# Second feed-forward with tokens sorted by expert through DRAM, and seven query-key products moved from GpSimd to VectorE

## Chip, cores and metric

The kernel runs on one core of a Trainium2 chip. The metric is the device time of one launch in microseconds, the median of three runs. TensorE (PE in the profile) multiplies matrices into PSUM banks, VectorE (DVE), ScalarE (ACT) and GpSimd (POOL) work elementwise, and SyncE (SP) issues the transfers. Each engine runs its own instruction list in order and meets the others at semaphores.

## The reference, cut to what matters

`x` holds 32 tiles of 128 tokens with 128 features, 4096 tokens in all. Eight residual steps follow each other: attention 0, feed-forward 0, attention 1, feed-forward 1, token attention, feed-forward 2, attention 3, feed-forward 3. The change concerns feed-forward 1 (eight experts of width 352, of which each token uses its best two) and, since they now stand beside it differently, token attention (16 heads of one token attend to each other) and feed-forward 2.

```python
# feed-forward 1, on layernorm(x): E = 8, I = 352, TOP_K = 2
logits = jnp.einsum('th,eh->te', xf, w_router)
probs = jax.nn.softmax(logits, axis=-1)
topw, topi = jax.lax.top_k(probs, TOP_K)
topw = topw / jnp.sum(topw, axis=-1, keepdims=True)
combine = jnp.einsum('tk,tke->te', topw, onehot)
gate = jax.nn.silu(jnp.einsum('th,eih->eti', xf, w_gate))
up = jnp.einsum('th,eih->eti', xf, w_up)
down = jnp.einsum('eti,ehi->eth', gate * up, w_down)
out = jnp.einsum('eth,te->th', down, combine)
# token attention, on layernorm(x): 16 heads of width 8, causal over the heads
scores = jnp.einsum('bsqd,bskd->bsqk', qh, kh) / math.sqrt(hd)
attn = jax.nn.softmax(jnp.where(mask, scores, -1e18), axis=-1)
out = jnp.einsum('bsqk,bskd->bsqd', attn, vh)
# feed-forward 2, on layernorm(x): 128 -> 512 -> 128, hidden layer and w2 rounded to fp8
```

## The kernel before

All of x stays in SBUF. Work goes in 32 tiles of 128 tokens, taken in 8 groups of 4 tiles (512 tokens). The order is written out by hand: each engine's block in `program` is one list, with a loop over pairs of groups for the middle of each stage (`walk`), and every hand-over is a wait on a counted semaphore.

Feed-forward 1 is dense. Its 8 x 352 = 2816 hidden units are cut into 22 chunks of 128 (`NC1`), and every group of 512 tokens goes through all 22 chunks, 176 chunks in all. For a chunk TensorE forms the gate (line 1199) and the up product (1205), each 512 columns in fp32, and adds the four 128x128 down products of the chunk two before (`finish`, 1181) into a bank that holds the group's sum. ScalarE applies silu (845), VectorE multiplies the two (`hide`, 1664). The router's weights come in by scaling the input of the up product (`shared`, 1654), or the hidden units where a chunk spans two experts (1672); their rows go through the DRAM tensor `share_rows` and come back broadcast over the partitions.

Token attention for the tiles of the group before runs between the chunks, at fixed slots of the 22 (`SCORE_SLOTS` and the like). For one tile GpSimd forms the query-key products (`products`, 647, four instructions), VectorE adds them up and prepares the softmax (`score`, 1727 to 1737), ScalarE takes the exponential (829), VectorE divides (`probabilities`, 1741 to 1747), GpSimd forms the products with the values (`weighted`, 660), and VectorE adds them into x (`combine`, 1753 and 1758). There is one buffer for each kind of products, so GpSimd may form the next tile's only once the last ones are read. GpSimd also does the two small operations of every inverse deviation (506, 508).

The last four tiles of token attention run in `feed_forward2`, one beside each of its groups 0 to 3. One group there is: `norm_stats` (1351, 1356) and `norm` (1374) on VectorE, four transposes (1122), four 512-column products (1225), `rectify` on ScalarE (867), sixteen fp8 products (1233), and two VectorE operations that add the result (1779, 1784). Groups 4 to 7 follow, with the start of attention 3 between them: its projections, the split of queries and keys into bf16 parts on GpSimd (515 to 529), and 18 transfers of those parts from SyncE's queue (377, 381), on which its first scores (964) wait.

Of the kernel before, what the change touches and what calls it, by code (L numbers as in the profile page):

```python
# [50 lines left out]
NC1 = E * I1 // P  # L51
EXPERTS1 = [((P * c) // I1, (P * c + P - 1) // I1) for c in range(NC1)]
MIXED = [c for c in range(NC1) if EXPERTS1[c][0] != EXPERTS1[c][1]]
FIRST1 = [min(c for c in range(NC1) if EXPERTS1[c] == (e, e)) for e in range(E)]
# [15 lines left out]
for _name, _len in (("bv0", 128), ("bv1", 128), ("bv3", 128), ("bo1", 128), ("bo3", 128), ("b_ffn0", 128),  # L70
                    ("b2_ffn2", 128), ("gate_b", E), ("first_wins", E), ("heads_causal", H * H)):
    ROWS[_name] = (_at, _at + _len)
    _at += _len
# [8 lines left out]
def waits_apart(eng):  # L82

    eng.nop(nofuse=True)
# [23 lines left out]
def program(nc, x_in, ctx_in, ctx_t, mask0, mask3, w_attn, w_ffn0, w_router, w_gate, w_up, w_down, w1, w2, gate3,  # L108
            mlp1, mlp2, mlp2_b, cols_in, rows_in, consts_in, pick_in, out):
    with ExitStack() as ctx:  # L110
# [3 lines left out]
        def sem(name):  # L114
# [57 lines left out]
        room = sb("room", [P, 2 * E * I1 + E * 3 * P])  # L172
        xn_all = room[:, 0:NT * P]
        wg = room[:, 0:E * I1]
        wu = room[:, E * I1:2 * E * I1]
        wd = room[:, 2 * E * I1:3 * E * I1].rearrange("p (c d) -> p c d", c=NC1)
# [20 lines left out]
        ctx_tok = [work[2 + b][:].rearrange("p (t d) -> p t d", t=TG) for b in range(2)]  # L197
        xq = h3
# [9 lines left out]
        hidden1 = [area[:, GT * i:GT * (i + 1)] for i in range(4)]  # L208
        xw = [area[:, GT * (4 + i):GT * (5 + i)] for i in range(2)]
        share = [q_rows[h][:].rearrange("p s n -> p (s n)").bitcast(F32).rearrange("p (e n) -> p e n", e=E // 2)  # L210
                 for h in range(2)]
        share_mixed = [ctxT[:, 0, :], ctxT[:, 1, :], xnT[:]]
        share_rows = nc.dram_tensor("share_rows", (2, E, GT), F32, kind="Internal").ap()
        zeros_b = sb("zeros_b", [P, P], BF16)
        comb1 = [sb(f"comb1{b}", [P, E, TG]) for b in range(2)]
# [21 lines left out]
            chunk_down xw_ready share_stored""".split()  # L237
# [9 lines left out]
         product_ready, lin_taken, x_first, x_second, rows_loaded, lin_ready, pick_loaded, chunk_down,  # L247
         xw_ready, share_stored) = (sem(n) for n in names)
        share_loaded = [sem(f"share_loaded{h}") for h in range(2)]
# [1707 lines left out]
```

## Time and profile before

| | us |
|---|---|
| median of three runs (1754.88 to 1757.84) | 1756.35 |
| the profiled execution: its own time | 1759.78 |
| the profiled execution: span, first to last instruction | 1757.7 |
| busy of the span: PE, DVE, ACT, POOL | 80%, 75%, 41%, 39% |

A profile describes one execution. "Busy" leaves out waiting and the issue of transfers. A view of windows gives each engine's busy time in a stretch; a timeline row gives start, duration, engine, line, operation and, in brackets, how long the engine had been idle and what released it; a view by line groups all instructions of a source line. The fp32 matmuls count as two instructions each ("x8" is four products of 128 columns).

### The profile page before, as it was taken

The numbers are of one execution on the slowest core, as the hardware profiler recorded it, in microseconds if no ns is written. First come the engines' busy times: TensorE is split into PE (matmuls) and PEld (weight loads), VectorE is DVE, ScalarE is ACT, GpSimd is POOL, SyncE is SP. The second block draws the span as 40 slices with busy tenths as digits, with TensorE's granted clock in tenths as the row PEclk, the third lists the DMA queues.
The fourth block names the chain that finished last, engine by engine and source line by source line (L and its number), as shares of the span: only waits on it lengthen the run. The fifth ranks groups of instructions, "written<-read, shape, count | busy, mean of one in ns | idle before, by whom it ended". The sixth has DMA issues, their size and how long they took to land. (4 is left out here: it accounts for less than half of the span.)

```text
span 1757.7 us, 32824 instructions
## 1 busy us (share of the span) xinstructions
PE 1407.4 (80%) x10456; PEld 897.4 (51%) x10456; DVE 1318.4 (75%) x3282; ACT 727.7 (41%) x1306; POOL 690.7 (39%) x718
## 2 busy tenths in 40 slices
PE   3888883489989998988988989565589897878787
PEld 1555552256666565554545545333266664455454
DVE  5768776676767569889788897877467564899898
ACT  1455552156656324334333343232166564333333
POOL 0223211023341024445354454454024431687786
PEclk9999996599999999999999999877699998899899
DMA  8455530364532221020220211000554450000000
GB/s 187 66 81 69 70 49 1 44 159 66 73 49 37 91 84 68 29 79 22 80 68 24 84 35 64 12 1 1 101 69 68 60 69 5 1 13 1 13 12 12
DMA packets 73205, 92.98 MB, mean 53 GB/s; under 512 B 7984, under 2 KB 59952, under 8 KB 70448
## 3 DMA queue, kind: packets, MB, share of 16 engines
q1 hardware_dynamic: 73072, 91.36, 26.6%
q8 instruction: 65, 1.06, 0.3%
q14 instruction: 68, 0.56, 0.1%
HBM read 51.35 MB, written 2.23 MB: 30 GB/s over the span
## 5 line engine op out<-in xcount | busy, mean ns | idle before, releaser
L1400 DVE TENSOR_REDUCE neg_max<-bank 128x4 f32<-128x512 f32 x384 | 252.7, 686 | 149.5 <-PE bank L966 147.7
L764 ACT ACTIVATE probs<-bank 128x512 f32<-128x512 f32 x384 | 212.3, 596 | 169.8 <-PE bank L993 169.0
L1181 PEld LDWEIGHTS bank<-room,area 128*128 128x128 f32 x1408 | 188.6, 195 | 83.9 <-issue 80.2
L845 ACT ACTIVATE work<-bank 128x512 f32<-128x512 f32 x176 | 105.1, 597 | 292.1 <-PE bank L1199 246.7
L964 PE MATMUL bank<-mask_b,ident_b 128*128 128x512 bf16 x384 | 155.9, 406 | 76.0 <-DMA k_rows<-area 50.5
L506 POOL TENSOR_SCALAR rstd_a<-meanvar 128x4 f32<-128x4 f32 x64 | 15.9, 249 | 457.9 <-DVE meanvar L1356 371.4
L660 POOL TENSOR_TENSOR prod<-mask_i,work 128x128 f32<-128x128 f32 (+3 forms) x128 | 133.7, 1075 | 157.9 <-DVE mask_i L1747 157.9
L1181 PE MATMUL bank<-room,area 128*128 128x128 f32 x1408 | 189.5, 279 | 0.0
L1199 PE MATMUL bank<-xT,room 128*128 128x512 f32 x352 | 183.0, 602 | 0.0
L1664 DVE TENSOR_TENSOR area<-work,bank 128x512 f32<-128x512 f32 x176 | 119.2, 682 | 56.7 <-PE bank L1205 50.5
L1205 PE MATMUL bank<-area,room 128*128 128x512 f32 x256 | 134.7, 608 | 28.4 <-DVE area L1664 16.8
L966 PE MATMUL bank<-k_rows,q_rows 96*128 96x256 bf16 x768 | 156.6, 287 | 0.0
L757 ACT ACTIVATE q_rows<-bank 32x512 bf16<-32x512 bf16 x192 | 103.0, 582 | 120.6 <-PE bank L976 116.9
L983 PE MATMUL bank<-ident_b,mask_b 128*128 128x512 bf16 x384 | 134.9, 393 | 3.0 <-ACT probs L764 1.8
L993 PE MATMUL bank<-q_rows,k_rows 128*128 128x128 bf16 x1536 | 135.9, 222 | 0.0
L647 POOL TENSOR_TENSOR probs<-h,work 128x128 f32<-128x128 f32 (+3 forms) x128 | 120.0, 967 | 23.4 <-DVE probs L1727 13.0
L993 PEld LDWEIGHTS bank<-q_rows,k_rows 128*128 128x128 bf16 x1536 | 112.5, 100 | 27.8 <-issue 2.2
L1007 PE MATMUL bank<-probs,v_aug 128*32 128x128 f32 x3072 | 112.9, 288 | 0.8
L515 POOL CAST area<-area 128x1024 bf16<-128x1024 f32 x19 | 19.7, 1036 | 227.6 <-DMA k_rows<-area 170.2
L966 PEld LDWEIGHTS bank<-k_rows,q_rows 96*128 96x128 bf16 x768 | 78.6, 102 | 54.0 <-issue 11.2
L585 POOL TENSOR_TENSOR probs<-probs,work 128x512 f32<-128x512 f32 x64 | 82.5, 1289 | 50.1 <-DVE probs L1854 50.1
L1205 PEld LDWEIGHTS bank<-area,room 128*128 128x128 f32 x256 | 46.7, 191 | 99.8 <-issue 42.4
(182 smaller groups left out, 2789.2 us busy)
## 6 DMA issues: line engine op xcount, KB each, us to landing
q_rows<-area SPq DMA_DIRECT2D x144, 128.0 KB
k_rows<-area SPq DMA_DIRECT2D x288, 64.0 KB
q_rows<-share_rows SPq DMA_DIRECT2D x16, 1024.0 KB, 4.6
ctxT<-ctx_t SPq DMA_DIRECT2D x24, 256.0 KB, 7.7
ctxT<-share_rows SPq DMA_DIRECT2D x32, 128.0 KB, 3.7
ctxT<-share_rows SPq DMA_DIRECT2D x16, 192.0 KB, 3.6
xnT<-share_rows SPq DMA_DIRECT2D x16, 192.0 KB, 3.5
mask_i<-mask SPq DMA_DIRECT2D x8, 256.0 KB, 8.5
```

Of the source, the lines that this page charges most:

```text
L647: ins = pool.tensor_tensor(prod[:, at:at + 4 * nj * DH].rearrange("p (i j d) -> p i j d", i=4, j=nj), q[:, 4 * i:4 * i + 4, :].unsqueeze(2 ...
L660: ins = pool.tensor_tensor(prod2[:, at:at + 4 * nj * DH].rearrange("p (i d j) -> p i d j", i=4, d=DH), tok_p[:, 4 * i:4 * i + 4, 0:nj].uns ...
L764: act.activation(probs[j].rearrange("p a b -> p (a b)"), T_BANK[j % 2][:], ACT.Exp).then_inc(exp_done, 1)
L964: pe.matmul(dst[:], ident_b[:], bcast(mask(b, t), 4), start=True, stop=False)
L966: mm = pe.matmul(dst[:, 256 * i:256 * i + 256], q_rows[b][SCORE_ROWS, 2 * j + i, tok], k_rows[b][SCORE_ROWS, :, 2 * j + i, tok], start=Fal ...
L983: pe.matmul(T_BANK[j % 2][:], mask(b, t), bcast(ident_b[:], 4), start=True, stop=False)
L993: mm = pe.matmul(dst[:, i * P:(i + 1) * P], k_rows[b][:, j % 2, hp, tok], q_rows[b][:, hp, tok], start=False, stop=i == 3)
L1181: mm = pe.matmul(dst[:, t * P:(t + 1) * P], hidden1[(c + 2 * b) % 4][:, t * P:(t + 1) * P], wd[:, c, :], start=False, stop=c == NC1 - 1 an ...
L1199: pe.matmul(S_BANK[c % 2][:], wg[:, P * c:P * (c + 1)], xT[b][:], start=True, stop=True).then_inc(gate_filled, 1)
L1205: pe.matmul(T_BANK[c % 2][:], wu[:, P * c:P * (c + 1)], xT[b][:] if mixed else xw[e % 2], start=True, stop=True).then_inc(up_filled, 1)
L1400: dve.tensor_reduce(neg_max[:, 4 * j:4 * j + 4], S_BANK[j % 2][:].rearrange("p (h k) -> p h k", h=4), AX.X, ALU.max, negate=True).then_inc ...
L1664: ins = dve.tensor_tensor(h, work[c % 2][:], T_BANK[c % 2][:], ALU.mult)
```

## The change

Feed-forward 1 computes only the two chosen experts of each token. The tokens are taken in 4 chunks (`NCH`) of 8 tiles (1024 tokens, 2048 token-expert pairs). For a chunk:

- `route_stats`, `route_norm`, `logits` and `choose` (VectorE, TensorE) find the two experts and, after a tanh on ScalarE, the weights; `ranks` counts with 17 bf16 products, for each pair, how many earlier pairs have the same expert; `put` turns that into the row of each pair and into the expert of each block, in some twenty small VectorE steps.
- `scatter` (GpSimd) writes the normalised rows into the DRAM tensor `moe_rows` with 16 indirect transfers of 128 rows of 512 bytes. Each expert's rows begin at a multiple of 128, so 24 blocks of 128 rows (`NBLK`) always suffice, 96 for all chunks (`NB`). `clear_rows` zeroes the tensor beforehand, 6.3 MB, in four transfers issued at the start of feed-forward 0.
- `sorted_rows` (SyncE) loads four blocks at a time (a quad, 24 steps in all) and stores the results over them. Per block TensorE transposes the rows (one of the quad's four), forms gate and up with the tokens as weights and the expert's 352 columns as the moving side, transposes the hidden units in three pieces and forms three down products. The expert is read into a register once a quad and sets the address of the weights.
- `gather` (GpSimd) fetches for each group two rows per token with 8 indirect transfers, and `add_taken` (VectorE) adds them to x with the weights, 8 instructions.

Token attention starts at step 9 of the 24 (`FIRST_STEP`), one tile a step: tiles 0 to 14 beside the blocks, tiles 15 to 31 behind them. For tiles 1, 3, 5, 7, 9, 11 and 13 (`ON_DVE`) VectorE forms the query-key products itself. Feed-forward 2's groups 0 to 6 stand beside the tiles 15 to 30, group 7 behind the last tile. The start of attention 3 now stands beside tiles 21 to 23; its split is made by VectorE, and its 18 transfers are issued then. This part is written out without loops.

```diff
+UNITS = [(0, P), (P, P), (2 * P, I1 - 2 * P)]
+TC = 2 * TG
+NCH = NT // TC
+QUAD = 4
+NQ = 6
...
+FIRST_STEP = 9
+ON_DVE = [n for n in range(NK - FIRST_STEP) if n % 2]
...
+        FFN2_STATS = {15: 0, 16: 1, 17: 2, 18: 3, 20: 4, 24: 5, 28: 6}
+        FFN2_NORM = {16: 0, 17: 1, 18: 2, 19: 3, 21: 4, 25: 5, 29: 6}
+        FFN2_ADD = {17: 0, 18: 1, 19: 2, 20: 3, 22: 4, 26: 5, 30: 6}
+        NEXT_STATS = {21: 0, 22: 1}
+        NEXT_NORM = {22: 0, 23: 1}
...
+            def sorted_rows():
+                sp.wait_ge(t_filled, 8 * NT)
...
+                def load(k):
+                    if k % NQ == 0:
+                        sp.wait_ge(scattered[k // NQ], 16 * 2 * TC)
+                    if k >= 4:
+                        sp.wait_ge(blk_turned, k - 3)
...
+            def scatter(c):
+                pool.wait_ge(placed, c + 1)
...
+                for o in range(2 * TC):
+                    t = o // 2
+                    pool.indirect_dma_start(
+                        moe_rows, bass.IndirectOffsetOnAxis(place_i[:, c, o:o + 1].bitcast(mybir.dt.uint32), 0),
+                        rows_of(c, t // TG)[:, t % TG, :], None).then_inc(scattered[c], 16)
...
+                at = 3 * NG
+                for n in range(NT):
+                    g, t = divmod(n, TG)
+                    if n + 1 < NT:
+                        products(n + 1)
+                    for events in (FFN2_STATS, NEXT_STATS):
+                        if n in events:
+                            at += 1
+                            inv_std(at)
+                    weighted(n)
+                    if g + 1 < NG:
+                        if t < 2:
+                            gather(g + 1, range(2 * t, 2 * t + 2))
+                        if t == 2:
+                            token_std(g + 1)
...
+                def experts(k):
...
+                    four = pe.value_load(expert_i[0:1, c, q:q + 1], min_val=0, max_val=E ** QUAD - 1)
...
+                    pe.matmul(S_BANK[i % 2][:, 0:I1], tokens, room[:, bass.ds(weights_at[k, m], I1)], start=True, stop=True
+                              ).then_inc(gate_filled, 1)
...
+                for n in range(NK - FIRST_STEP, NT):
+                    score(n)
+                    combine_last(n)
+                    between(n)
+                    if n in FFN2_ADD:
+                        ffn2_add(FFN2_ADD[n])
+                    if n in FFN2_NORM:
+                        ffn2_norm(FFN2_NORM[n])
...
+                    probabilities(n)
+                    if n == 23:
+                        for part in range(4):
+                            attention(2, True, part)
+                combine(NT - 1)
+                norm_stats(NG - 1, NT, tok_written)
+                ffn2_norm(NG - 1)
+                ffn2_add(NG - 1)
...
             def score(n):
 
-                dve.wait_ge(tok_products, n + 1)
+                if n in ON_DVE:
...
+                        ins = dve.tensor_tensor(
+                            prod[:, at:at + 4 * nj * DH].rearrange("p (i j d) -> p i j d", i=4, j=nj),
+                            q[:, 4 * i:4 * i + 4, :].unsqueeze(2).to_broadcast([P, 4, nj, DH]),
+                            k[:, 0:nj, :].unsqueeze(1).to_broadcast([P, 4, nj, DH]), ALU.mult)
```

In the order of the instructions, three places. First TensorE, one chunk of the dense stage before (`bank` is PSUM, `room` the experts' weights, `area` hidden units or scaled tokens):

```order
L1199 MATMUL bank<-xT,room 128x512 [waits gate_act]
L1205 MATMUL bank<-area,room 128x512 [waits hidden_ready]
L1181 MATMUL bank<-room,area 128x128 [waits hidden_ready]
L1181 MATMUL bank<-room,area 128x128 x3
```

and the start of a quad with one block now:

```order
L1302 TENSOR_LOAD m2b
L1302 ISA x2
L1313 REGISTER_ALU [waits gate_act,blk_taken]
L1313 ISA
L1313 MATMUL bank<-room,area 128x352
L1317 ISA [waits hidden_ready]
L1317 MATMUL bank<-room,area 128x352
...
L1325 MATMUL bank<-ident,area 128x128 [waits hidT_taken,hidden_ready]
L1325 MATMUL bank<-ident,area 128x128
L1325 MATMUL bank<-ident,area 96x128
L1334 ISA [waits hidT_taken]
L1334 MATMUL bank<-room,area 128x128
```

Two long products and four short ones of a chunk became two shorter long ones, three transposes and three short ones of a block, with an address instruction (ISA) ahead of each product and a load of the quad's experts ahead of its first.

Second GpSimd, between two tiles of token attention, before:

```order
L647 TENSOR_TENSOR probs<-h,work 128x512
L506 TENSOR_SCALAR rstd_a<-meanvar 128x4 [waits stats_ready]
L508 TENSOR_TENSOR rstd<-rstd_a,minus_half 128x4 [waits pool_steps]
L660 TENSOR_TENSOR prod<-mask_i,work 128x128 [waits tok_summed,tok_probs]
```

and now, at tile 16:

```order
L556 TENSOR_SCALAR rstd_a<-meanvar 128x4 [waits stats_ready]
L558 TENSOR_TENSOR rstd<-rstd_a,minus_half 128x4 [waits pool_steps]
L748 TENSOR_TENSOR prod<-mask_i,q_rows 128x128 [waits tok_summed,tok_probs]
...
L748 TENSOR_TENSOR prod<-mask_i,q_rows 128x512
L595 DMA mask_b<-moe_rows,m2b 128x128 [waits x_mixed,blk_stored0,blk_stored1]
L595 DMA mask_b<-moe_rows,m2b 128x128 x3
L734 TENSOR_TENSOR probs<-h,q_rows 128x128 [waits tok_scored,xq_ready]
```

Four indirect transfers stand between the products of one tile and the next, at two of every four tiles.

Third VectorE, at tile 18, where one tile, the gathered rows of group 5 and a group of feed-forward 2 meet:

```order
L2058 TENSOR_REDUCE mask_i<-prod 128x32 x3
L2063 SCALAR_TENSOR_TENSOR x<-mask_i,gates,x 128x128 [waits tok_summed]
L1885 SCALAR_TENSOR_TENSOR x<-mask_b,m2b,x 128x128 [waits gathered5]
...
L1894 BN_STATS m2b<-x 128x6 [waits x_mixed]
...
L2010 TENSOR_TENSOR o<-bank,b_q 128x512 [waits x_written,down_filled]
L2014 SCALAR_TENSOR_TENSOR x<-o,gates,x 128x512 [waits down_read]
L1510 TENSOR_SCALAR xn<-x,meanvar,rstd 128x128 [waits rstd_ready,f_filled]
...
L2046 TENSOR_REDUCE mask_i<-probs 128x16 [waits tok_exp]
```

Before, x got the dense stage's sum in one instruction a group (line 1678); the eight of line 1885 take its place.

## Rows read from the trace of the kernel before

**Rows 1.** Windows by stage: start:end, length, busy (instructions) per engine, PEclk, DMA.

```profile
333.50:576.60 243.10, 209.24 (x2381) 144.30 (x2382) 166.16 (x425) 137.87 (x281) 66.23 (x75) 0.92 0.43 76
...
576.60:1127.30 550.70, 492.72 (x2213) 303.26 (x2211) 453.77 (x1006) 195.02 (x282) 242.70 (x253) 0.98 0.17 56
...
1127.30:1242.00 114.70, 61.30 (x246) 34.49 (x246) 82.79 (x217) 32.55 (x50) 52.13 (x60) 0.73 0.03 8
```

**Rows 2.** Timeline of TensorE in the dense stage: start, us, engine, line, count.

```profile
704.71 1.05 PE L1181 MATMUL bank<-room,area 128*128 128x128 f32 x8
705.60 1.02 PE L1199 MATMUL bank<-xT,room 128*128 128x512 f32 x2
```

**Rows 3.** VectorE by line, 576 to 1127 us: count, busy us, mean ns, idle before.

```profile
L1664 DVE TENSOR_TENSOR area<-work,bank 128x512 f32<-128x512 f32 x176 | 119.2, 682 | 56.7 <-PE bank L1205 50.5 <-issue 2.9 <-PE bank L1181 1.2
...
L1727 DVE TENSOR_REDUCE probs<-probs 128x16 f32<-128x128 f32 (+1 forms) x112 | 46.4, 475 | 4.2 <-POOL probs L647 4.2
...
L1753 DVE TENSOR_REDUCE mask_i<-prod 128x32 f32<-128x128 f32 (+1 forms) x108 | 44.8, 476 | 15.0 <-POOL prod L660 15.0
...
L1732 DVE TENSOR_TENSOR probs<-probs,rows 128x256 f32<-128x256 f32 x28 | 27.6, 986 | 1.0
...
L1737 DVE TENSOR_TENSOR probs<-probs,mask_i 128x256 f32<-128x256 f32 x28 | 27.1, 966 | 1.0
...
L1747 DVE TENSOR_TENSOR mask_i<-probs,mask_i 128x256 f32<-128x256 f32 x28 | 11.9, 425 | 1.4 <-DVE mask_i L1743 0.5
...
L1735 DVE TENSOR_REDUCE mask_i<-probs 128x16 f32<-128x256 f32 x28 | 11.8, 420 | 1.0
...
L1741 DVE TENSOR_REDUCE mask_i<-probs 128x16 f32<-128x256 f32 x28 | 11.6, 413 | 0.0
...
L1758 DVE SCALAR_TENSOR_TENSOR x<-mask_i,gates,x 128x128 f32 (+1 forms) x27 | 9.5, 352 | 1.0
...
L1743 DVE RECIPROCAL mask_i<-mask_i 128x16 f32<-128x16 f32 x28 | 7.1, 253 | 1.0
```

**Rows 4.** Timeline around the last group of feed-forward 2.

```profile
1218.38 0.60 PE L1122 MATMUL bank<-ident,xn 128*128 128x128 f32 x4
...
1229.82 1.11 PE L1122 MATMUL bank<-ident,xn 128*128 128x128 f32 x4 [5.43 <-DVE xn L1374]
...
1241.28 0.75 DVE L1784 SCALAR_TENSOR_TENSOR x<-o,gates,x 128x512 f32<-128x512 f16 x1
...
1258.36 0.58 PE L964 MATMUL bank<-mask_b,ident_b 128*128 128x512 bf16 x1 [13.10 <-DMA k_rows<-area]
```

**Rows 5.** The page: busy tenths of the 16 DMA engines in 40 slices.

```profile
DMA  8455530364532221020220211000554450000000
```

**Rows 6.** Timeline of SyncE's queue: a DMA issue.

```profile
350.04 0.44 SPq L413 DMA_DIRECT2D room<-w_down  x1
```

**Rows 7.** DMA issues: count, KB each, us to landing.

```profile
work<-ctx_in SPq DMA_DIRECT2D x8, 256.0 KB, 2.8
```

**Rows 8.** GpSimd by line, 576 to 1250 us.

```profile
L660 POOL TENSOR_TENSOR prod<-mask_i,work 128x128 f32<-128x128 f32 (+3 forms) x128 | 133.7, 1075 | 157.9 <-DVE mask_i L1747 157.9
L647 POOL TENSOR_TENSOR probs<-h,work 128x128 f32<-128x128 f32 (+3 forms) x128 | 120.0, 967 | 23.4 <-DVE probs L1727 13.0 <-DVE h L1374 10.3
L508 POOL TENSOR_TENSOR rstd<-rstd_a,minus_half 128x4 f32<-128x4 f32 x25 | 27.9, 1117 | 2.1
```

**Rows 9.** Timeline of VectorE where feed-forward 1 ends.

```profile
1131.22 0.87 DVE L1351 BATCH_NORM_STATS2 stats<-x 128x6 f32<-128x128 f32 x4
...
1134.12 1.11 DVE L1374 TENSOR_SCALAR h<-x,meanvar,rstd 128x128 f32<-128x128 f32 x4 [1.54 <-POOL rstd L508]
...
1138.52 3.31 DVE L1374 TENSOR_SCALAR xn<-x,meanvar,rstd 128x128 f32<-128x128 f32 x4 [1.54 <-POOL rstd L508]
```

**Rows 10.** ScalarE by line, 576 to 1250 us: loads of a function table.

```profile
L845 ACT ACT_TABLE_LOAD x29 | 37.2, 1283 | 5.1 <-DVE area L1664 5.0
```

**Rows 11.** Waits, 1127 to 1235 us: total us, times, longest.

```profile
DVE o L1779 <- PE bank L1233: 18.4, 6, 6.4
```

More of the change, by code:

```diff
@@ L352, in load_rest @@
                 load_x(4, 4, x_loaded)
+                sp.dma_start(work[3][:, 0:P], consts_in[2]).then_inc(upper_loaded, 16)
                 sp.dma_start(mask3_i[:], mask3).then_inc(loaded2, 16)
@@ new lines, in gather @@
+            def gather(g, tiles):
+                for b in range(2):
+                    pool.wait_ge(blk_stored[b], 16 * NQ // 2 * (g // 2 + 1))
+                if g >= 2:
+                    pool.wait_ge(x_mixed, TG * (g - 1))
+                waits_apart(pool)
+                for t in tiles:
+                    for k in range(2):
+                        o = 2 * (TG * (g % 2) + t) + k
+                        pool.indirect_dma_start(
+                            taken(g, t, k), None, moe_rows,
+                            bass.IndirectOffsetOnAxis(place_i[:, g // 2, o:o + 1].bitcast(mybir.dt.uint32), 0)
+                        ).then_inc(gathered[g], 16)
@@ L572, in body @@
                                 add_bias(TG * (gr - 1) + t)
+                        if a == 1 and left == 0:
+                            route_std(1)
+                            scatter(0)
                 pool.wait_ge(setup_dve, 2)
@@ L1444, in attention @@
                 xc = NT * BLOCK[a]
+                if part is not None:
+                    if part < 3:
+                        split(0, part)
+                    else:
+                        take_v(0, 0)
+                    return
                 if start:
@@ new lines, in add_taken, with token_stats @@
+            def add_taken(g):
+                dve.wait_ge(gathered[g], 16 * 2 * TG)
+                c = g // 2
+                for k in range(2):
+                    for t in range(TG):
+                        xt, n = tile(TG * g + t), TG * (g % 2) + t
+                        ins = dve.scalar_tensor_tensor(xt, taken(g, t, k), weight[:, c, k, n:n + 1], xt, ALU.mult, ALU.add)
+                    if k == 0:
+                        step(ins)
+                ins.then_inc(x_mixed, TG)
+            def token_stats(g):
+                dve.wait_ge(x_mixed, TG * (g + 1))
+                for t in range(TG):
+                    ins = dve.bn_stats(t_stats[:, t, :], tile(TG * g + t))
+                step(ins)
+                for t in range(TG):
+                    ins = dve.bn_aggr(t_meanvar[:, t, :], t_stats[:, t, :])
+                ins.then_inc(t_stats_ready, 1)
```

1176 lines of the change are left out of this document (640 added, 536 removed).

## The prediction

> **What bounds the kernel now.** Read the windows by stage first [rows 1]. The dense feed-forward takes 550.7 us, and TensorE is busy for 492.7 of them at a granted clock of 0.98 of the upper level, 2.4 GHz; VectorE follows with 453.8. The next window, 114.7 us, holds the last four tiles of token attention and feed-forward 2, and there no engine is full: VectorE 82.8, TensorE 61.3. The timeline of TensorE shows what the dense stage consists of [rows 2]: a chunk's four down products take 0.89 us from start to start, a 512-column product 0.86, so a chunk 2.61, and 176 of them 459 us. The rest of the 550.7 is waiting, part of it on VectorE, whose own waits on the up product are 50.5 us [rows 3]: the two run hand in hand. Last, after feed-forward 2 TensorE stands still for 13.1 us, until the transfers of the split keys have landed, and the first scores of attention 3 start at 1258.36 [rows 4]. So the change is weighed against one stretch: 576.6 to 1258.4, **681.8 us**. What lies before it and after it keeps its instructions, but for a few named below. The clearing of the DRAM rows, 6.3 MB, is issued where attention 0 ends. There the DMA engines are idle for the whole seventh slice and busy for three tenths of the ones beside it, 44 us each [rows 5], and I cost it at nothing. Even at 2.8 us for 256 KB, one after the other [rows 7], it would be 69 us; without that cover some 30 of them would stand before attention 1's own transfers.
>
> **Until the first block.** The positions of chunk 0 are formed two tiles before attention 1 ends. That stage has 32 tiles in 243.1 us [rows 1], 7.6 each, so this is 15 us before the end, at 561.6. 17 counting products and eleven small VectorE steps take some 4.5, and GpSimd then issues 16 indirect transfers. No trace shows one. Bounds: an issue on SyncE's queue holds it for 0.44 us [rows 6]; if GpSimd stayed until a transfer has landed, 2.8 more [rows 7], 3.2 in all. Its nearest kin is a GpSimd operation on four elements, 1.12 [rows 8], and I take 1.3, since it must also form 128 addresses. 16 are 21 us; add two landings of 2.8 (scatter, then the load of the quad) and 1.5 for the first transposes and their copy: the first block's products start at 594, **17.5 us** into the stretch. Bounds 4 and 48.
>
> **The blocks: 96 for 176 chunks.** Gate and up with 352 columns are 0.59 each by [rows 2], 1.18; three down products of 0.222 are 0.67; four transposes (three of hidden units, one of rows) are 0.16 each, four having taken 0.60 to the end of the last [rows 4], 0.64. A block is 2.49, a quad 9.96. For the register load and address work per quad I take 1.0; the trace has no load into a register, so nothing from below and one landing, 2.8, from above. The Trainium skill (DMA: Bandwidth & Descriptors, Latency and other measured facts) puts the floor of such a load at some 600 ns; with that price alone each quad would be 0.4 us shorter. No row here shows it. A step is 11.0 us while TensorE is the bound. That holds for the first nine, where VectorE has only products of hidden units and routing: 99 us. Routing of chunks 1 to 3 adds, on TensorE, three times eight router products (0.38 each, between one and two of the 128-column products, 9), five transposed groups (3) and the counting (5), and waits on VectorE's chains of 13 and 20 small steps, three times some 5.3, 16. Together **132 us**; bounds 110 and 160.
>
> **Steps 9 to 23, one tile of token attention each.** VectorE's work per tile is the sum of [rows 3] other than line 1664: 4 x 0.475 + 0.986 + 0.420 + 0.966 + 0.413 + 0.253 + 0.425 + 4 x 0.476 + 0.352 = 7.6. Four products of hidden units, 0.52 each (0.68 for 512 columns [rows 3]), are 2.1. In seven of the fifteen tiles it forms 1280 products per partition as well: at 682 ns per 512 that is 1.7 bare, and 3.0 beside GpSimd, 1.4 on average. Per group it adds the gathered rows (8 x 0.352), measures and normalises (1.25 and 1.11 [rows 9]): 5.2, a quarter of it per tile, 1.3. The exponential now comes between silus, and a table load is 1.28 us each way [rows 10]; 0.9 of that is left uncovered. Sum 13.3, above TensorE's 11.0 and above GpSimd's: 4.3 for the value products, 3.87 in 8 of 15 tiles for the others [rows 8], two gathers a tile 2.6, the deviation 0.3, in all 9.3. So VectorE sets the pace: **200 us**. From below TensorE's 165; from above 230, if every hand-over costs 2 us more. This is also what the seven moved products do: they take 27 us from an engine with room and give VectorE 21, which has none.
>
> What the two engines cost each other is in [rows 9]: four normalisations take 1.11 us where GpSimd rests and 3.31 where its products run, 0.55 more each.
>
> **Tiles 15 to 31.** VectorE: 17 tiles, 129.5. Seven groups of feed-forward 2, each 0.69 + 0.75 for the result, 1.25 measuring, and 2.2 normalising (between 1.11 and 3.31, since GpSimd hardly rests here), 34. Gathered rows of groups 5 to 7 and four normalisations, 21. Start of attention 3, 6.9 for two groups, 5.2 for the split and the values, 2.4 for clearing, 14.5. Busy 199. Waits: the result of feed-forward 2 comes later than VectorE asks, 18.4 us in 6 cases before [rows 11]; four of the seven groups stand in successive tiles, 12. In the six tiles with gathers GpSimd needs 4.3 + 3.87 + 5.2 + 1.35 = 14.7 and VectorE some 12: 16. The last group is bare: value products and sum of tile 31, 6.6; measuring and normalising, 4.0 with GpSimd's share; then the chain from the transposes at 1229.82 to the end of the add at 1242.03 [rows 4], 12.2. In all 199 + 12 + 16 + 22.8 = **250 us**, bounds 215 and 285. The transfers of the split keys now start at tile 23, 80 us before they are needed, so the 16 us from that add to the first scores shrink to **1.5**.
>
> **The sum.** 17.5 + 132 + 200 + 250 + 1.5 = 601, against 681.8: 80.8 less. The profiled span goes from 1757.7 to 1676.9. The median was 1.35 below the profiled span, so the forecast is 1675.5, **1676 us**, a ratio of 0.954. TensorE's gain is much larger than that (96 x 2.49 = 239 us for 459), but VectorE and GpSimd keep all of token attention, and it can only start once the first experts are back, at step 9.
>
> **The rivals.**
> A, fewer conflicts: GpSimd has seven sets of products less, so the two additions of 986 and 966 ns fall to the 420 of their uncontended kin, 35 us over 32 tiles, and the gathers hide, 16 us. It gives 1625. For it speaks that VectorE's idle time in the dense stage was mostly TensorE's doing; against it, that GpSimd is busier in the tail than it ever was.
> B, more conflicts: all of some 220 two-operand and normalising operations in steps 9 to 23 and the tail pay the 0.55 us of [rows 9], 121 us, less 25 already counted and a third that falls into waits anyway: +60, 1736. Beside it stands a rule of the Trainium skill (SBUF — State Buffer, Who interferes with whom): the two engines share a port pair that one holds for a whole instruction, and a transfer issued from GpSimd starves while VectorE copies or normalises; it tells of one that went from 620 to 3100 ns. By that price alone each gather beside a normalisation would be 2.5 us later, and all 24 of the tail 60 us, which would put the sum at 1736 too; the trace has no such transfer, but its normalisations, 1.11 and 3.31, agree with the lock.
> C, slower: GpSimd is held by each indirect transfer until it has landed. Exposed are the 16 of chunk 0 and the 24 gathers of the tail, 40 x (c - 1.3). The gain of 81 is gone at c = 3.3 us; at 3.7 (0.44, a landing of 2.8 and its own 0.5) the time is 1772. For it: tile 4g+2 cannot add before its eight gathers are in. Against it: the semaphore is raised by the transfer, and nothing in GpSimd's list waits on it.
> D, the work does not shrink in effect: the seven moved products and the added rows fill what the blocks free, 33 us in steps 9 to 23 and 46 in the tail. It gives 1755, within 0.2%. No row points to it.
>
> **How the numbers follow.** Chances: forecast 0.52 (its own range 1645 to 1710), A 0.24, B 0.14, C 0.08, D 0.02. The range 1620 to 1745 takes in the forecast, most of A, and B. A measurement of this kernel can tell 0.2%, 3.5 us, from no change: faster 0.90, same 0.02, slower 0.08.
>
> **What would show it.** In the profile after: TensorE's first 352-column product near 594; quads 11 us apart up to step 8 and 13.3 from step 9, VectorE busy over 90% in the latter; the indirect transfers 1.3 us apart on GpSimd's queue; 250 us from the last block to the last add of feed-forward 2, and first scores within 2 us of it. Wrong would be quads further than 13 us apart before step 9 (the register load, or the loads from DRAM), a queue of GpSimd over 3 us per gather, or first products after 610.

## The result

The changed kernel takes 1660.4 us (median of 4 runs, 1654.7 to 1666.5) against 1756.9 (4 runs, 1754.9 to 1757.8): a ratio of 0.945, 95% interval [0.942, 0.949]. The forecast was 1676. The profiled execution of the changed kernel has a span of 1652.8 us, against 1757.7 before; it is the fastest of the four, so its span lies 24.1 us under the span forecast, the median 15.6 under its own.

The stretch that the prediction weighed is counted from 576.6 in both. It ended at 1258.4 before; now the first scores of attention 3 start at 1156.2, so it takes 579.6 us where 681.8 were and 601 were forecast. What lies behind it takes 496.6 us, before 499.3. Here are windows of the profile after by stage (busy time and instructions of PE, PEld, DVE, ACT and POOL, then the granted clock as a share of full speed, the DMA share and GB/s): until the first block's product, nearly all of steps 0 to 8, steps 9 to 23, and from there to the last add of feed-forward 2.

```profile
576.60:591.30 14.70, 2.86 (x13) 2.05 (x13) 1.08 (x4) 0.88 (x3) 8.32 (x11) 0.64 0.33 100
...
591.30:686.00 94.70, 88.67 (x570) 69.62 (x570) 45.67 (x177) 44.16 (x91) 54.30 (x56) 0.98 0.31 90
691.00:897.00 206.00, 167.31 (x837) 120.11 (x838) 164.15 (x386) 111.89 (x194) 122.28 (x130) 0.89 0.18 50
...
897.00:1155.20 258.20, 83.84 (x274) 41.26 (x272) 196.25 (x488) 39.87 (x67) 174.96 (x191) 0.62 0.11 25
```

Step 9's first product starts at 690.9. Beside the forecast:

| part | forecast, us | profile after |
|---|---|---|
| to the first block's product | 17.5 | 14.7 |
| steps 0 to 8 | 132 | 99.6 |
| steps 9 to 23 | 200 | 206 |
| tail, to the last add | 250 | 258 |
| to the first scores | 1.5 | 1.1 |

So four of five terms hold within 8 us, and the fifth, steps 0 to 8, was 32 us too long. The two terms behind it were 14 too short, so that 21 us of error are left in the sum: part of the closeness of the total is luck. TensorE is nearly full in steps 0 to 8 (88.7 of 94.7). In steps 9 to 23 none is: TensorE 81%, VectorE 80% (forecast over 90%), GpSimd 59%.

What a block is made of is seen in TensorE's timeline after (start, duration, engine, line; rows from one quad where nothing waits; a row can hold several instructions that follow each other):

```profile
781.23 0.60 PE L1294 MATMUL bank<-ident,q_rows 128*128 128x128 f32 x4
781.67 0.49 PE L1325 MATMUL bank<-ident,area 128*128 128x128 f32 x3
782.00 0.83 PE L1334 MATMUL bank<-room,area 128*128 x6
782.67 0.76 PE L1313 MATMUL bank<-room,area 128*128 x2
783.26 0.75 PE L1317 MATMUL bank<-room,area 128*128 x2
783.85 0.49 PE L1325 MATMUL bank<-ident,area 128*128 128x128 f32 x3
```

From start to start the gate product takes 0.59, the up product 0.59, three transposes 0.33, the down products 0.67, and once per quad the four transposes of rows (L1294) 0.44. A block is 2.29 us, a quad 9.2. The register load and the indirect scatters of chunk 0 follow, each a line of its source's view (count, min/median/max in ns, first and last start):

```profile
L1302 PEldq TENSOR_LOAD <-m2b x24: 296/300/493, 589.5 to 885.2; - x24
```

```profile
L581 POOL DMA_INDIRECT moe_rows<-work,m2b x16: 954/958/1304, 564.8 to 584.1; - x16
```

The sixteen scatters of chunk 0 start 1.29 us apart (1.3 forecast), 0.96 of it an instruction and some 0.30 a gap. The view of transfers gives the other scatters' median time from issue to landing:

```profile
moe_rows<-q_rows,m2b POOLq DMA_INDIRECT x48, 2.3
```

What VectorE waits for after, first in steps 9 to 23, then in the tail (releaser, us in total, times, longest):

```profile
DVE area L1916 <- PE bank L1317: 20.6, 13, 3.1
DVE x L1885 <- DMA ctxT<-moe_rows,m2b: 9.3, 2, 7.5
DVE area L1916 <- ACT work L918: 7.0, 6, 2.5
DVE probs L2032 <- POOL probs L734: 3.0, 1, 3.0
```

```profile
DVE mask_i L2058 <- POOL prod L748: 14.9, 9, 3.9
DVE o L2010 <- PE bank L1388: 14.1, 4, 10.2
DVE probs L2032 <- POOL probs L734: 10.2, 4, 4.2
DVE x L1885 <- DMA qbT<-moe_rows,m2b: 7.8, 2, 4.5
DVE x L1885 <- DMA work<-moe_rows,m2b: 4.6, 1, 4.6
```

Rows of before that answer to them are [rows 3] and [rows 11]. The end of the stretch after; in [rows 4] the first scores had waited 13.1 us for a transfer:

```profile
1154.37 0.75 DVE L2014 SCALAR_TENSOR_TENSOR x<-o,gates,x 128x512 f32<-128x512 f16 x1
1155.18 1.16 PE L1037 MATMUL bank<-wa,ctxT 128*128 128x128 f32 x8 [1.64 <-DVE x L2014]
1156.17 0.38 PE L1054 MATMUL bank<-mask_b,ident_b 128*128 128x512 bf16 x1
```

### The profile page after: what moved, and what is told of

Same layout as the page of the kernel before. It is cut to its first block and busy times, and to the rows that moved or that the text cites. A ratio compares the mean times of both kernels' runs of the same rounds, so it can differ in the third digit from the quotient of the medians.

```text
span 1652.8 us, 31331 instructions
## 1 busy us (share of the span) xinstructions
PE 1190.6 (72%) x9741; PEld 792.9 (48%) x9741; DVE 1195.9 (72%) x3162; ACT 699.9 (42%) x1333; POOL 770.4 (47%) x806
## 5 line engine op out<-in xcount | busy, mean ns | idle before, releaser
L607 POOL CAST area<-area 128x1024 bf16<-128x1024 f32 x36 | 37.6, 1043 | 218.9 <-DMA k_rows<-area 200.4
L1916 DVE TENSOR_TENSOR area<-work,bank 128x352 f32<-128x352 f32 x96 | 49.2, 516 | 86.0 <-PE bank L1317 78.9
L1212 PE MATMUL bank<-ident,xn 128*128 128x128 f32 x32 | 8.9, 432 | 122.7 <-DVE xn L1510 113.0
L1317 PE MATMUL bank<-room,area 128*128 x192 | 80.7, 505 | 20.7 <-DVE area L1916 20.7
L1244 PEld LDWEIGHTS bank<-room,area 128*128 128x128 f32 x512 | 69.0, 203 | 43.0 <-issue 20.3
L748 POOL TENSOR_TENSOR prod<-mask_i,v_aug 128x128 f32<-128x128 f32 (+1 forms) x64 | 64.0, 1032 | 53.5 <-DVE mask_i L2052 53.5
L1054 PEld LDWEIGHTS bank<-mask_b,ident_b 128*128 128x128 bf16 x384 | 37.8, 98 | 105.3 <-DVE neg_max L1536 39.2
L1334 PE MATMUL bank<-room,area 128*128 (+1 forms) x576 | 87.8, 292 | 0.7
L683 POOL TENSOR_TENSOR area<-probs,work 128x512 f32<-128x512 f32 x64 | 81.4, 1272 | 11.8 <-POOL probs L666 5.1
L1097 PEld LDWEIGHTS bank<-probs,v_aug 128*32 128x32 f32 x3072 | 82.8, 112 | 3.1 <-issue 1.4
## 6 DMA issues: line engine op xcount, KB each, us to landing
moe_rows<-m2b SPq DMA_DIRECT2D x4, 1536.0 KB, 13.3
```

What stands on the lines that cost most here:

```text
L683: pool.tensor_tensor(hidden[e % 2][:, 0, :], product[e % 2], work[2 + e % 2][:], ALU.mult).then_inc(hidden_ready, 1)
L1054: pe.matmul(dst[:], ident_b[:], bcast(mask(b, t), 4), start=True, stop=False)
L1097: mm = pe.matmul(O_BANK[32 * i:32 * i + 32, half * P:(half + 1) * P], v_aug[b][:].rearrange("p t h c -> p (t h c)")[:, at:at + 32], probs[ ...
L1317: pe.matmul(T_BANK[i % 2][:, 0:I1], tokens, room[:, bass.ds(weights_at[k, m] + I1, I1)], start=True, stop=True).then_inc(up_filled, 1)
L1334: mm = pe.matmul(R_BANK[:, m * P:(m + 1) * P], hid_t[i % 3][0:n, j * P:(j + 1) * P], room[0:n, bass.ds(weights_at[k, m] + 2 * I1 + P * j, ...
```

## The experiments

All start from the changed kernel. Its runs spread by 12 us, and in the profiles the first block's product starts anywhere from 591 to 604 us. Part of that scatter is there before the change's own work (attention 1's last output product starts at 577.8 in one profile of the same kernel and at 582.1 in another). So the profiles are compared by distances that do not contain it, and in the two profiles of the changed kernel these repeat to within 2 us. Two profiles are few: a difference of 2 us is taken for none, and one of 4 or 5 for a hint. "Quads 1 to 9" is the distance between the starts of the transposes (L1294) of quad 1 and of quad 9, and so on; these stand one step ahead of the quad's own products. The tail is taken from the last up product (L1317) to the start of the last add of feed-forward 2 (L2014). The ratio is to the kernel before, run beside each kernel, with its 95% interval.

| kernel | median us | ratio, interval | quads 1 to 9 | 9 to 23 | tail |
|---|---|---|---|---|---|
| changed, first profile | 1660.4 | 0.945 [0.942, 0.949] | 89.3 | 192.1 | 259.8 |
| after_again | 1660.0 | 0.945 [0.943, 0.948] | 89.5 | 193.8 | 260.0 |
| products_gpsimd | 1649.5 | 0.940 [0.938, 0.943] | 89.1 | 183.1 | 260.6 |
| products_vector | 1654.5 | 0.942 [0.940, 0.945] | 89.5 | 194.7 | 257.5 |
| two_units | 1658.4 | 0.945 [0.943, 0.947] | 84.2 | 196.1 | 258.0 |
| fixed_experts | 1661.0 | 0.943 [0.940, 0.945] | 87.1 | 192.8 | 260.0 |
| half_gathers | 1635.5 | 0.929 [0.927, 0.931] | 89.5 | 182.6 | 244.3 |
| spread_gathers | 1662.8 | 0.946 [0.944, 0.948] | 89.2 | 192.2 | 259.8 |
| first8 | 1685.1 | 0.959 [0.956, 0.963] | 97.7 | 224.3 | 242.7 |
| no_exp | 1660.1 | 0.945 [0.943, 0.948] | 89.2 | 190.0 | 258.2 |
| scatter_later | 1659.1 | 0.944 [0.940, 0.947] | 89.7 | 194.0 | 259.8 |
| late_adds | 1657.0 | 0.944 [0.941, 0.947] | 89.0 | 188.2 | 260.2 |
| three_on_vector | 1647.7 | 0.938 [0.936, 0.940] | 89.2 | 184.8 | 252.4 |

**after_again**, no edit.

> The changed kernel itself, to have its time and its trace on the chip on which the others of this set run. Its four times so far lie 0.7% apart (1654.7 to 1666.5 us), so steps of a few us need it beside them. Expected 1655 to 1667; quads 9.4 us apart without routing, 13.7 from step 9 on.

As expected. The mean pace from quad 9 to 23 is 13.8 us (13.7 in the first profile); quads 7, 8 and 9, which have no routing beside them, stand 9.4 apart. The distances from quad 9 on repeat roughly in fours, 16 / 13 / 11 / 13 us. The additions of a gathered group start 6 us ahead of a long one (13 to 14, 17 to 18, 21 to 22); in it, or from its very start, stand the group's normalisation and, with tile 3, 7 or 11, products that were moved to VectorE.

**products_gpsimd**: the second part of the change undone.

```diff
-ON_DVE = [n for n in range(NK - FIRST_STEP) if n % 2]
+ON_DVE = []
```

> All query-key products back on GpSimd (the list of tiles that VectorE forms is empty); nothing else. The prediction's theory, VectorE alone sets the pace of steps 9 to 23 and has no room for the seven moved products: 7 x 3.0 = 21 us less than the changed kernel, about 1640. Rival 1, from the trace of the changed kernel (VectorE 79% busy there, TensorE 82%, and each waits for the other): the pace is a chain through both, and a good part of the 21 falls into waits that exist anyway: 5 to 12 less, about 1652. Rival 2, the hand-over from GpSimd costs more than the products on VectorE: 3 to 8 us more, about 1666.

11 us less from quad 9 to 23, 10.5 in the median: rival 1. Seven tiles' products, 3.3 us each in the first profile of the changed kernel, left VectorE, 23 us, and half of that reached the end. The three long distances fell from 16.1, 16.3 and 16.5 to 12.1, 12.0 and 12.0, 13 us together, and the others grew by 2. So the saving stands where a group's additions and a tile's moved products follow each other, and the four moved tiles elsewhere show no cost; this is read from one profile, and no run moves them apart. Part of the other half is seen by lines (700 to 880 us; busy, mean ns). First the two lines that changed most, in the first profile of the changed kernel:

```profile
L2037 DVE TENSOR_TENSOR probs<-probs,rows 128x256 f32<-128x256 f32 x13 | 7.5, 579 | 0.4
L2052 DVE TENSOR_TENSOR mask_i<-probs,mask_i 128x256 f32<-128x256 f32 x13 | 6.8, 522 | 0.4
```

In after_again the first of them took 775 ns, the second again 522. Now with all products on GpSimd, where its work stands beside VectorE's for longer:

```profile
L2037 DVE TENSOR_TENSOR probs<-probs,rows 128x256 f32<-128x256 f32 x14 | 14.0, 1002 | 0.5
...
L2052 DVE TENSOR_TENSOR mask_i<-probs,mask_i 128x256 f32<-128x256 f32 x14 | 12.6, 900 | 0.5
```

**products_vector**: the opposite.

```diff
+ON_DVE = list(range(1, NK - FIRST_STEP))
```

> VectorE forms the products of all tiles 1 to 14 (fourteen in place of seven), GpSimd those of tile 0 and of tiles 15 to 31. The prediction's theory (VectorE alone sets the pace): 7 x 3.0 = 21 us more, 1681. Rival 1 (a chain through both engines): 5 to 12 more, 1669. Rival 2 (the hand-over is the dear part): 3 to 8 less, 1655.

The prediction's theory wanted 21 us more; from quad 9 to 23 it is 0.9 more. The median, 5.5 less, is rival 2's number, but its interval overlaps that of the changed kernel, products_gpsimd spoke against rival 2, and the stretch where it should act did not get shorter. So none of the three theories is borne out. The lines here, and the products themselves (L2024), which had taken 828 and 832 ns each in the first profile of the changed kernel:

```profile
L2024 DVE TENSOR_TENSOR probs<-h,v_aug 128x128 f32<-128x128 f32 (+3 forms) x28 | 18.9, 733 | 0.0
...
L2037 DVE TENSOR_TENSOR probs<-probs,rows 128x256 f32<-128x256 f32 x13 | 5.5, 425 | 0.4
L2042 DVE TENSOR_TENSOR probs<-probs,mask_i 128x256 f32<-128x256 f32 x13 | 5.5, 425 | 0.4
...
L2063 DVE SCALAR_TENSOR_TENSOR x<-mask_i,gates,x 128x128 f32<-128x128 f32 x12 | 4.2, 351 | 0.4
```

Four instructions of a tile (L2037, L2042, L2063 and L2052, here 424 ns) cost 1.6 us here, 3.1 with all products on GpSimd, and 2.4 to 2.7 in the two profiles of the changed kernel. A tile's products moved to VectorE so cost their 2.9 less what they free beside them. From half to all moved that is 20 us of new work against 11 to 15 freed in these four and 3 to 6 in the products moved before, an estimate from these means, and the stretch agrees with it.

**two_units**: less work for TensorE alone.

```diff
-                    for j, (at, n) in enumerate(UNITS):
+                    for j, (at, n) in enumerate(UNITS[:2]):
```

(and the same in the down product)

> Left out of each of the 96 blocks: the transpose and the down product of the third unit of 96 hidden values (output incomplete). VectorE's and ScalarE's work is untouched. TensorE has 0.13 + 0.22 = some 0.35 us less per block, 1.4 per quad. The prediction's theory: steps 0 to 8 get 1.4 shorter each, 12 us, steps 9 to 23 not at all, since VectorE alone sets their pace: 1648. Rival (a chain through both engines): steps 9 to 23 get shorter too, by 0.7 to 1.4 each, 10 to 20 us more: 1630 to 1638.

This tests whether TensorE sets the pace. Quads 7 to 9 stand 8.2 to 8.3 apart in place of 9.4, and of quads 9 to 23 nothing is saved, 196.1 against 193.8. That is the number of the prediction's theory; the rival's 10 to 20 us are not there. The 12 us expected in steps 0 to 8 did not come in full: quads 1 to 9 take 5.3 less, and the median, 1658.4, is 1.6 less, within the scatter. Where TensorE's saving goes is seen in its waits (690 to 905 us), the two lines of which were 20.7 and 14.2 us in the first profile of the changed kernel:

```profile
PE bank L1317 <- DVE area L1916: 28.1, 12, 7.7
PE bank L1325 <- ACT area L924: 18.3, 14, 1.6
```

and in its granted clock from 700 to 880 us, 0.85 here (first window) and 0.92 in after_again (second); it was 0.89 in the first profile:

```profile
700.00:880.00 180.00, 134.14 (x555) 89.41 (x556) 144.61 (x338) 92.53 (x162) 104.08 (x110) 0.85 0.16 44
```

```profile
700.00:880.00 180.00, 144.35 (x730) 103.55 (x731) 147.97 (x340) 97.50 (x170) 105.72 (x112) 0.92 0.16 45
```

TensorE is busy for 10 us less of the 180, and the quads come no faster, so it is not what holds them. How much of its relief the lower clock took back no run separates.

**fixed_experts**: the register load left out.

```diff
-                    four = pe.value_load(expert_i[0:1, c, q:q + 1], min_val=0, max_val=E ** QUAD - 1)
...
+                        weights_at[k, j] = (QUAD * q + j) // 3 * EXPERT_W
```

> The register load of a quad and its address arithmetic are left out: TensorE takes each block's weights at fixed addresses (wrong experts for many rows, the same work). The prediction put 1.0 us per quad on this: quads without routing would go from 9.4 us apart to 8.4, 9 us in steps 0 to 8. Rival, from the trace after (the load 0.30 us, the arithmetic 0.15, no idle time of TensorE put down to either): 9.4 stays 9.4 within 0.1, and the prediction's 11.0 was too long because of its block of 2.49 us, not only because of the load. The median would be 1660 within its scatter of 6.

Quads 7 to 9 are 9.2 apart, and quads 1 to 9 take 2.4 us less: 0.2 to 0.3 us per quad, a quarter of the 1.0 forecast. The rival's 0.1 was a little low, its reading right.

**half_gathers**: 32 of 64 indirect gathers left out.

```diff
-                    for k in range(2):
+                    for k in range(1):
...
-                        ins = dve.scalar_tensor_tensor(xt, taken(g, t, k), weight[:, c, k, n:n + 1], xt, ALU.mult, ALU.add)
+                        ins = dve.scalar_tensor_tensor(xt, taken(g, t, 0), weight[:, c, k, n:n + 1], xt, ALU.mult, ALU.add)
```

> Of each token's two expert rows only the first is fetched, and it is added twice, with either weight (output wrong by that): 32 of 64 indirect gathers less, at 1.25 us of GpSimd each, VectorE's work unchanged. The prediction (exposed in the tail alone, 16 us for 24 gathers; in steps 9 to 23 GpSimd has room): 8 us less, all of it after the last block. Rival 1, from the trace after (VectorE stands before its additions until a gather lands, in the steps as well, and TensorE behind it): 15 to 25 less, a third of it in steps 9 to 23. Rival 2 (gathers are hidden): 0.

24.4 us less in the median than after_again, three times the prediction's 8: rival 1. In the tail it is 15.7 us for 12 gathers, 1.3 each, their whole time on GpSimd. From quad 9 to 23 it is 11 us, of which 6.2 between quads 9 and 10 (15.5 to 9.3). That is step 8, where VectorE stands before the first additions, with the next product of hidden units queued behind them, in after_again:

```profile
689.47 0.52 DVE L1916 TENSOR_TENSOR area<-work,bank 128x352 f32<-128x352 f32 x1 [1.66 <-PE bank L1317]
697.32 2.32 DVE L1885 SCALAR_TENSOR_TENSOR x<-ctxT,m2b,x 128x128 f32<-128x128 f32 x8 [7.34 <-DMA ctxT<-moe_rows,m2b]
699.56 0.51 DVE L1916 TENSOR_TENSOR area<-work,bank 128x352 f32<-128x352 f32 x1
```

So relief of GpSimd moves these steps as much as relief of VectorE did in products_gpsimd.

**spread_gathers**: the gathers of groups 5 to 7 two to a tile.

```diff
+                    if n < 14 and t < 2:
+                        gather(g + 1, range(2 * t, 2 * t + 2))
+                    if 14 <= n < 26:
+                        gather((n + 6) // TG, [(n + 6) % TG])
```

> Same work, other places: the gathers of groups 5 to 7, two bursts of four in successive tiles before, now two in each of four tiles and up to two tiles earlier. If the bursts cause VectorE's waits in the tail (on landing rows 14.6 us, and on products of GpSimd queued behind the bursts 10.2): 10 to 18 us less between the last block and the last addition. Rival (GpSimd's total work in the tail is what VectorE waits for, wherever it stands): 0 to 3.

Nothing gained: the rival's number. But not by the rival's way alone. The windows of the tail, of after_again and of this kernel:

```profile
898.30:1158.30 260.00, 85.49 (x283) 42.34 (x281) 196.10 (x491) 42.06 (x73) 177.51 (x194) 0.62 0.11 25
```

```profile
903.40:1163.20 259.80, 83.17 (x283) 41.55 (x281) 204.98 (x490) 41.71 (x72) 178.01 (x194) 0.61 0.11 25
```

VectorE is busy for 8.9 us more with the same instructions, and waits that much less. The waits for landed rows fell from 15.3 to 7.9 us and those for products from 10.2 to 3.2, with 5.4 of new ones for GpSimd's deviation, now queued behind gathers. But its adds of feed-forward 2 went from 759 to 1364 ns in the mean of seven (the longest took 3.17 us), and its normalisations from 537 to 671. The reading that fits is that GpSimd now runs beside them: a wait was turned into a conflict.

**first8**: token attention one step earlier.

```diff
-FIRST_STEP = 9
+FIRST_STEP = 8
...
+                gather(0, range(TG))
                 scatter(2)
                 scatter(3)
-                gather(0, range(TG))
```

> Token attention starts at step 8 in place of 9, so the tail has 16 tiles in place of 17; feed-forward 2's first four groups move one tile later with it; the gathers of group 0 go ahead of the scatters of chunks 2 and 3 on GpSimd. The prediction's account (a tile costs a step of TensorE's pace 2.3 to 4.3 us and saves a tail tile of 14 to 15): 10 us less, 1650. Rival: the rows of chunk 0 are not back in time, step 8 waits for the gathers, 3 to 8 us of the gain are lost: 1655. If the tail's first tiles are held by feed-forward 2 rather than by their own work, nothing is gained.

25 us slower, and for a reason of my edit: the deviation of group 0 stood behind the 32 scatters that I had moved back, and VectorE waits for it once, for 36.4 us. The tail did lose a tile's 17 us. The distance from quad 8 to 9 is 18.1 here, 8.7 more: VectorE waits 9.0 us for the first gathered rows, a step earlier than in after_again, where it waits 7.3. Whether a clean version gains is open.

```profile
DVE h L1904 <- POOL m2b L566: 36.4, 1, 36.4
```

**no_exp**: ScalarE without changes of table in steps 9 to 23.

```diff
-                act.activation(tok_e, tok_s, ACT.Exp, scale=DH ** -0.5).then_inc(tok_exp, 1)
+                func = ACT.Copy if n < NK - FIRST_STEP else ACT.Exp
+                act.activation(tok_e, tok_s, func, scale=DH ** -0.5).then_inc(tok_exp, 1)
```

> In steps 9 to 23 the exponential of token attention is replaced by a copy on the same 128x256 elements, so that ScalarE keeps one table (wrong probabilities): 30 table loads of 1.28 us and nothing else leave. The prediction put 0.9 us per step on them: 13 us less in steps 9 to 23, 1647. Rival 1 (VectorE's chain hides them, though TensorE's trace shows 14 us of waiting for ScalarE's copy of hidden units): 0 to 3 less. Rival 2 (each pair of loads stands in a chain through all three engines): 2.6 each, 30 or more less.

2 to 4 us less from quad 9 to 23, where 13 were forecast: rival 1. TensorE's waits there after (691 to 897 us) and without the exponential (690 to 905):

```profile
PE bank L1317 <- DVE area L1916: 20.7, 9, 4.4
PE bank L1325 <- ACT area L924: 14.2, 15, 1.3
```

```profile
PE bank L1318 <- DVE area L1917: 39.3, 19, 5.7
```

The 14.2 us are gone, and the wait for VectorE has nearly doubled. VectorE in turn is busy for 153.9 of the 180 us from 700 to 880, against 148.0 in after_again and 144.3 in the first profile, with no work added: part of the relief came back as longer instructions.

**scatter_later**: the scatters of chunk 3 behind the first gathers.

```diff
+                    if n < 4:
+                        scatter(3, range(4 * n, 4 * n + 4))
```

> Same work: the gathers of group 0 go ahead of the sixteen scatters of chunk 3 on GpSimd, and these follow four at a time behind the value products of tiles 0 to 3. In the trace of the changed kernel VectorE stands 7.3 us in step 8 until the first gathered rows land, since GpSimd issues the scatters of chunk 3 ahead of them. Expected: that wait goes, the distance from quad 9 to quad 10 falls from 15.5 to 10, 5 to 6 us less in all. Rival: the scatters, 1.25 us each, now delay GpSimd's products in tiles 0 to 3 by 5 us each and cost as much or more: 0 to 10 us more.

Both came true, and cancel. Quad 9 to 10 falls from 15.5 to 9.4; then quad 12 to 13 takes 22.4, and 9 to 23 is unchanged.

**late_adds**: the additions of a group behind the fourth product of hidden units.

```diff
-                        between(n)
+                        between(n, (3,))
                         probabilities(n)
                     hide(QUAD * k + 3)
+                    if n >= 0:
+                        between(n, (2,))
```

> Same work: in steps 9 to 23 the additions and the statistics of a gathered group move from between VectorE's second and third product of hidden units... to behind the fourth, where nothing stands. If the pace is set by how VectorE's work lies between those products (TensorE can be ahead by two blocks only) and by the wait for gathered rows: the steps of 16.4 us, every fourth, fall to 13 or 14, 8 to 12 us less. Rival (the amount of work sets the pace, wherever it stands): 0.

4 to 5 us less from quad 9 to 23, half of what was expected, and the median, 3 less, is within the scatter. Nor did the distances fall that were expected to: the long ones are 16.8, 14.9 and 18.0. So the place of VectorE's work between the products may count for a few us, but the mechanism expected is not shown.

**three_on_vector**: late_adds, and

```diff
+ON_DVE = [18, 22, 26]
```

> The changed kernel with two edits of placement, the work complete: the additions of a gathered group in steps 9 to 23 stand behind the fourth product of hidden units (as in late_adds, 5 us), and VectorE forms the query-key products not in seven tiles of the steps but in three tiles of the tail, 18, 22 and 26, whose products stand on GpSimd between two bursts of four gathers. Steps 9 to 23 should take 178 to 183 us by the segments (192 to 194 in the changed kernel, 183 with all products on GpSimd). In the tail VectorE waits 2.8 and 4.2 us for these products and 4.5, 4.6 and 3.3 for the rows gathered behind them. If GpSimd's queue is what ends these waits: 260 falls to 250 or 254, the median to about 1638. Rival, seen with the gathers spread (waits of 9 us left VectorE and its instructions grew by 9): 260 stays 260, the median is about 1644.

In the tail 7.6 us less, 252.4, within what GpSimd's queue was said to be worth. In steps 9 to 23 184.8, above the 178 to 183 expected and no better than the 183.1 of products_gpsimd alone: the 5 us of late_adds do not add to it, the long distances are 15.5, 14.9 and 15.6 where products_gpsimd has 12, and the median stays 10 us above the 1638 expected. At 1647.7 us it beats the changed kernel by 0.7% with all of the work done, and by the intervals it can't be told from products_gpsimd (1649.5).

## Why the prediction was right, and where it was not

**Until the first block**, 17.5 forecast, 14.7 measured. Of the 2.8 us little can be made: in after_again the same term is 18.8, and what repeats is the 13.4 and 13.3 us from attention 1's last output product. The scatters came 1.3 us apart as taken, and land in 2.3 us, not 2.8. Rival C falls with that: GpSimd is not held until a transfer has landed.

**Steps 0 to 8**, 132 forecast, 99.6 measured. Three terms were too large. Transposes at 0.16 each, read as the time to the end of the last of four; they follow each other at 0.11, which with the rest makes a quad 9.16 and not 9.96: 7 us over nine. The register load and its address work, 1.0, was a guess between bounds of 0 and 2.8 where no row stood; it is 0.2 to 0.3: some 7. The Trainium skill's floor for such a load (DMA: Bandwidth & Descriptors, Latency and other measured facts), some 600 ns, was nearer than my figure. The trace does not agree with it: the instruction takes 300 ns. And routing: 9 quads at 9.4 are 84.4, so it took 15 where 33 were forecast, 18 us; TensorE waits for VectorE's chains only 4.0 us (three times before L1275), where I had put 16. By the prediction's own sign, quads over 13 us apart before step 9 were to mean a dear register load or late loads from DRAM. Two distances are 13.2 and 13.3, and both are routing: quads without it stand 9.4 apart.

**Steps 9 to 23**, 200 forecast, 206 measured, the pace 13.3 against 13.7. The size is right by luck, by two errors that cancel. VectorE is busy for 10.9 us a step, not 13.3: two of a tile's additions, 986 and 966 ns before [rows 3], are 594 and 573 here, and the 0.9 for tables is no work of VectorE's. These make 1.7 of the 2.4; the rest I have not laid out. In their place come 2.8 us a step of waiting that the sum did not have. The step of the prediction that failed here is that VectorE's work alone sets the pace. What two_units and no_exp show is that neither TensorE nor ScalarE sets it: 1.2 us a quad off the one and 30 table loads of 1.28 us off the other leave quads 9 to 23 within 4 us of 193. VectorE's work counts, but at half: 23 us off it gave 11. GpSimd's queue counts too: 20 gathers less in these steps and just before them gave another 11, of which 6 are VectorE's one wait for the first rows. So the pace is set by a chain in which both stand. How VectorE can be idle for a fifth in it is argued, not shown: it takes its work in order, TensorE can be only two blocks ahead of its products of hidden units, and these stand close together at the end of a step and far apart in it. late_adds, 4 to 5 us, is a hint of this and no more; the full account of the 42 us of waiting is open.

**The moved products.** I wrote that they take 27 us from an engine with room and give VectorE 21, which has none. Undone, they give back 11. The direction was right, the price half. A tile's products cost VectorE 2.9 us in products_vector and 3.3 and 3.7 in the two profiles of the changed kernel, less what the neighbours gain when GpSimd is quiet. So this part of the change costs 0.6%, and the sorted rows bring the whole gain, and more.

**The tail**, 250 forecast, 258 measured. VectorE's busy time was well placed (199 and part of the last group forecast, 196 in all), its waits were not: 16 us for 24 gathers, and half_gathers gives 1.3 us for each one left out, 31 if that holds for all 24. Of rival A, the conflicts did fall in steps 9 to 23 (594 and 573 ns) but not in the tail, where L2037 and L2042 still take 876 and 928. Rival B, more conflicts, would have shown as VectorE busier than forecast; it is less busy in both parts. Rival D needs the gain of the blocks to be eaten up, and 102 us of it are there.

**The gap to attention 3** closed as forecast, 1.5 against 1.1.

Of the port that VectorE and GpSimd share, the Trainium skill (SBUF — State Buffer, Who interferes with whom) says that one engine holds it for a whole instruction. VectorE's durations agree: in the trace after, the same add (L2063) takes 352 ns in the median and up to 2264, its mean in steps 9 to 23 is 818, and in products_vector it is 351 (700 to 880 us). The other part of that rule, a transfer issued from GpSimd that starves while VectorE copies or normalises, does not show at the prediction's size, 2.5 us a gather and 60 in the tail: the 24 gathers of the tail land in 2.4 us at least, 2.6 in the median and 4.7 at most, with 0.94 to 1.09 us for the instruction.

## What to carry to other kernels

When several engines hand a small piece of work round, find what paces them by taking work off each in turn: what moves the end is in the chain, however idle it looks, and it can be more than one. Here TensorE and ScalarE were not in it, VectorE and GpSimd were. An operation that is moved between two engines that slow each other should be priced with its neighbours' durations, at no, half and full move: here half cost 11 us, and the second half nothing that can be told. A queue of indirect transfers on a computing engine can count at its full issue time where somebody waits for that engine, as it did in the tail here, so count the transfers first.

## What the hardware showed that I had not expected

- A load of 4 bytes into a register of TensorE's queue took 0.30 us, and the address arithmetic behind it 0.15; with both left out, a quad was 0.2 to 0.3 us shorter.
- An indirect transfer of 128 rows of 512 bytes took 0.96 us of GpSimd and a gap of 0.30; it landed after 2.3 us, and the next did not wait for it.
- Waiting and conflict were exchanged: with the gathers spread, some 9 us less of VectorE's waiting became 8.9 us more of busy time with the same instructions.
- Less work for TensorE in the steps where it waits for VectorE came with a lower granted clock, 0.85 against 0.92 and 0.89 in the two profiles of the changed kernel.
